# Feed-forward first: the order of TensorE's work in the steps shared by attention and feed-forward

## The reference

```
x = x + cross_attention(layernorm(x), ctx, ctx)       # 16 heads of 8
l = layernorm(x)
e = argmax(l @ Wr.T + br)                             # one of 8 experts for each token
x = x + (relu(l @ W1[e].T + b1[e]) @ W2[e].T + b2[e]) # 128 -> 512 -> 128
```

## Time and profile before

| what | us |
|---|---|
| median of 3 runs | 507.33 (504.11 to 508.76) |
| the profiled execution | 510.14 |
| its span | 508.3 |
| TensorE busy | 464.8 (91%) |
| VectorE busy | 408.4 (80%) |
| ScalarE busy | 314.4 (62%) |
| GpSimd busy | 240.2 (47%) |

### The profile page before, as it was taken

One profiled execution on the slowest core, in us unless ns is written; L12 is line 12 of the kernel. 1 busy time (PEld: TensorE's weight loads), 2 busy tenths in 40 slices (PEclk: granted clock), 3 DMA queues, 4 the chain that ended last, 5 costly groups with the idle time before them and its releaser, 6 DMA issues.

```text
span 508.3 us, 18979 instructions
## 1 busy us (share of the span) xinstructions
PE 464.8 (91%) x6467; PEld 349.6 (69%) x6468; DVE 408.4 (80%) x1061; ACT 314.4 (62%) x589; POOL 240.2 (47%) x390
## 2 busy tenths in 40 slices
PE   3999968899999999999999999979796989999991
PEld 1665634466666666666666666669686989999991
DVE  4999864678899998999989989878674768777871
ACT  1777755666656666666666666566464667767770
POOL 1558521222232845727447275357575444544552
PEclk9999997999999999999999999999998999999996
DMA  8455300001110211102111039132222322222220
GB/s 276 126 153 149 88 8 16 16 16 22 21 19 17 55 27 35 46 17 50 33 30 50 18 76 373 39 84 64 59 71 65 86 80 69 65 58 72 62 58 0
DMA packets 32745, 33.89 MB, mean 67 GB/s; under 512 B 6675, under 2 KB 26006, under 8 KB 32416
## 3 DMA queue, kind: packets, MB, share of 16 engines
q1 hardware_dynamic: 27840, 24.10, 18.0%
q0 software_dynamic: 4832, 8.80, 5.2%
HBM read 19.14 MB, written 9.99 MB: 57 GB/s over the span
## 4 chain that ended last, share of the span: by engine, by line
PE 58%; DVE 14%; issue 10%; DMA 3%; SPq 2%; ACT 2%; POOL 1%; DVEq 0%; POOLq 0%; ACTq 0%
PE PS L916 10%; PE PS L875 10%; PE PS L1022 10%; PE PS L1035 9%; PE PS L992 5%; PE PS L1001 4%; DVE MX L696 4%; PE PS L946 2%; PE PS L950 2%; PE PS L957 2%; PE PS L1007 1%; PE PS L905 1%; DMA BIG<-rows 1%; ACT PT L527 1%; DVE RD L700 1%
## 5 line engine op out<-in xcount | busy, mean ns | idle before, releaser
L449 POOL TENSOR_TENSOR VP<-BIG,C 128x128 f32<-128x128 f32 x128 | 56.3, 463 | 132.8 <-PE PS L1001 128.4
L696 DVE TENSOR_REDUCE MX<-PS 128x16 f32<-128x1024 f32 x64 | 78.3, 1223 | 28.7 <-PE PS L875 27.4
L916 PEld LDWEIGHTS PS<-C,SB 128*128 128x128 f32 x512 | 54.4, 142 | 67.9 <-ACT SB L544 32.4
L471 POOL DMA_INDIRECT out<-SB,BIG x71 | 70.0, 985 | 64.5 <-DVE SB L847 57.9
L916 PE MATMUL PS<-C,SB 128*128 128x128 f32 x512 | 84.8, 289 | 7.6 <-ACT PT L527 7.2
L544 ACT ACTIVATE SB<-SB 128x1024 f32<-128x1024 f32 x64 | 67.7, 1057 | 23.1 <-DVE SB L704 21.5
L1022 PE MATMUL PS<-BIG,KM 128*128 128x128 f32 x568 | 80.7, 282 | 0.7 <-issue 0.2
L704 DVE TENSOR_TENSOR SB<-PS,MX 128x1024 f32<-128x1024 f32 x64 | 77.4, 1210 | 1.7
L1035 PE MATMUL PS<-KM,SB 128*128 x568 | 76.1, 277 | 0.6 <-ACT SB L561 0.6
L1022 PEld LDWEIGHTS PS<-BIG,KM 128*128 128x128 f32 x568 | 71.6, 193 | 3.8 <-issue 3.1
L464 POOL DMA_INDIRECT rows<-X,DESTI x64 | 63.7, 995 | 22.3 <-issue 15.5
(11 more groups left out here) (123 smaller groups left out, 694.0 us busy)
## 6 DMA issues: line engine op xcount, KB each, us to landing
BIG<-rows SPq DMA_DIRECT2D x71, 66.0 KB
X<-in_x SPq DMA_DIRECT2D x16, 256.0 KB, 3.3
PT<-in_ctxT SPq DMA_DIRECT2D x16, 256.0 KB, 2.9
KM<-BIG SPq DMA_DIRECT2D x240, 16.0 KB
BIG<-in_we SPq DMA_DIRECT2D x1, 2576.0 KB, 10.2
KM<-in_w SPq DMA_DIRECT2D x1, 2048.0 KB, 14.6
out<-SB,BIG POOLq DMA_INDIRECT x71, 2.3
rows<-X,DESTI POOLq DMA_INDIRECT x64
```

The lines of the kernel that those rows point to most:

```text
L449: last = nc.gpsimd.tensor_tensor(dst, v, own, ALU.mult)
L471: nc.gpsimd.indirect_dma_start(out=out, out_offset=bass.IndirectOffsetOnAxis(ap=RT[:, s.r, ID:ID + 1].bitcast(i32), axis=0), in_=YO[:, s.r ...
L696: nc.vector.tensor_reduce(MX[:, n % 2, :], sc, axis=AX.X, op=ALU.max).then_inc(mx_done, 1)
L916: last = nc.tensor.transpose(bank(4)[:, i * P:(i + 1) * P], SB[:, n % 3, hp * P:(hp + 1) * P], ident)
```

## The change

In the loop over the shared steps TensorE's two calls are exchanged. The wait for the last reciprocals (`rd_done`) stays ahead of the feed-forward part of k = 2. Other engines' programs are the same.

```
@@ -1046,10 +1046,10 @@
             pe.wait_ge(tab_ready, 1)
             for n in range(F0, STEPS):
                 k = n - F0
-                stage2(Step(n // ST, n % ST, ST))
                 if k == 2:
                     pe.wait_ge(rd_done, NG)
                 ffn(0)(Step(k // RR, k % RR, RR))
+                stage2(Step(n // ST, n % ST, ST))
             steps(pe, STEPS - F0, NB1, RR, ffn(0))
```

## The result

The changed kernel takes 515.86 us (512.78 to 518.55, 6 runs), the kernel before 507.54 (503.83 to 508.76, 6 runs): ratio 1.017, 95% interval 1.0131 to 1.0209. A second series gave 515.72 against 506.68, ratio 1.0185 (1.0147 to 1.0224). The forecast was 514.9 us and a ratio of 1.015.

A forecast was written before the change was run, and what follows sets the result against it. TensorE was taken as the bound in steps 69 to 74, with DEST of step 77 gating the end. Terms 2.5 + 7.1 - 2.0 gave +7.6 us on the 507.33 median: 514.9 us, range 512.2 to 517.8, 8 in 10 508.5 to 518.7.

The forecast's parts named there:

- TensorE is the bound in steps 69 to 74: From 341.50 to 354.40 us TensorE is busy 12.90 of 12.90 us and nobody makes it wait.
- DEST is the point that counts: VectorE's DEST of step 77, the last routing batch, gates DESTI, home(10), load 18 and the blocks behind.
- Term 1: Steps 69 to 72: turns where TensorE and VectorE wait for each other take 17.57 us instead of 10.48, +7.1 us.
- the ring: Shared steps 69 to 72: L946, OT, RN, L836, relu, W2, next L946 wait in turn; 3.92 us per odd step.
- Term 2: Step 68, getting into the ring: T(1) and W1(0) come ahead of OT's counting matmuls; step 69's L946 is later, +2.5 us.
- Term 3: From step 73, getting out of the ring: pauses vanish, -3.69, but two waits partly remain; -2.0 us, between -3.7 and -1.1.
- +7.6 goes through to the end: Behind the last routing batch: DEST's whole delay of +7.6 us reaches the kernel's end through home(10) and load 18.
- the wait for block 18 stays near 3 us: Sign at TensorE behind the shared steps: its 3.12 us wait for block 18 stays about the same.
- the absorbed rival: TensorE's waits for blocks 17 and 18 take up delay if load 18 hangs elsewhere; 7.6 becomes 3.4, 510.7 us; chance 0.10.
- The clock rival: Clock falls to 1.2 GHz in the ring, steps 69 to 76: +11 us more, 526 us; chance 0.06.
- The signs: Steps 69 to 72: TensorE busy about two thirds, OT 4 us apart; home(10) near 388.4; pauses of steps 75 to 77 gone.

The follow-up runs named there:

- e8: Kernel before plus four unused VectorE copies ahead of the feed-forward part of steps 70 to 73; RN(0) to DEST 31.02 us against 30.73.
- e5: Changed kernel with VectorE adding the bias of block k-1 instead of k-2 in shared steps; 525.32 us, ratio 1.0328.
- e4: Kernel before with feed-forward first on TensorE only in steps 73 to 80; 508.64 us, ratio 1.0008.
- e11: Kernel before up to step 74; from step 75 T and W1 ahead of the step's waits, W2 behind; 505.17 us, ratio 0.9966.
- e6: Changed kernel with GpSimd writing home(k-3) ahead of the step's routing work instead of behind it; 514.59 us, ratio 1.0133.
- e7: Changed kernel plus four unused VectorE copies ahead of the feed-forward part of steps 70 to 73; RN(0) to DEST 45.78 us against 39.76.
- e10: Changed kernel with only W2 ahead of the step's own products, T and W1 behind them; RN(0) to DEST 42.72 us in one profile.
- e3: Kernel before with feed-forward first on TensorE only in steps 67 to 72; 514.09 us, ratio 1.0103.

## Why the prediction was right, point by point

- **TensorE is the bound in steps 69 to 74 and DEST is the point that counts**: held. e8's cheap copies show the first, the step from DEST to DESTI to home(10) the second (+9.04, +8.8). Over all fourteen profiles RN(0) to DEST runs from 28.9 to 48.1 us, while T(32) follows DEST by 49.0 to 53.4 us in each.
- **Term 1, the ring, +7.1**: 17.63 us against 17.57 forecast, +7.15. The links were right within 0.1 to 0.2 us, and that they add up to within 0.06 is luck: W2 to the next product was 0.99 us in each turn and not 0.89, relu of step 72 began 0.1 late, and the table arithmetic and the turn without L946 took 0.2 to 0.3 less than forecast. The sentence that T and W1 "end before relu does, so they add nothing" was wrong: they were put at about 1.0 us from RN's start on and took 1.75 (0.40 to T, 0.16 to W1, 1.19 to W2), as much as the way over L836 and relu. That made no difference to term 1, but e5 failed on it.
- **Term 2, +2.5**: step 69's L946 came 340.73 - 331.52 = 9.21 us behind RN(0) instead of 6.49, +2.7. The delay of OT was 5.74 - 4.54 = 1.20 us, as forecast, though no row shows the restart of 0.2 in it by itself; the 0.2 that was missing is W1 of step 69, which ended behind relu.
- **Term 3, -2.0**: wrong in size. From the first product of step 73 to the end of DEST it is 12.92 us instead of 13.75, -0.8, outside my bounds of -3.7 and -1.1, and done alone it even costs 1.1 (e4). I took the 3.69 us of pauses as something that vanishes and charged two turns at two thirds; pauses of 0.60, 0.67 and 0.60 us stayed, and the turns cost more than both in full (-1.1). TensorE waited there for results that VectorE hands over after its own feed-forward part, and W2 ahead of the counting delays the very next result. With only T and W1 in the pauses the gain is real, -1.84 (e11).
- **"+7.6 goes through to the end"**: wrong. DEST moved by 9.0, the end by 5.6 and 5.7 in the profiles at full clock. The load of block 18 got faster by 1.6 to 2.1 us, for a reason that I did not settle (3.92 and 3.45 before, 1.83 and 1.86 after). The clock, which fell behind the wait for block 18 before (W1 1.92 us; waits of 3.12 and 2.60 us), stayed up behind the shorter wait (1.19 and 1.12); that the shorter wait is why is not shown, as in e11 it stayed up behind 2.62. What should have been as it was, "the wait for block 18 stays near 3 us", was not. So a third of the loss was given back, but not as the absorbed rival had it: load 18 came late by all of the 8.8 us.
- **The clock rival**: I gave 0.06 to a clock that falls in the ring in every execution. It falls in some: one of three profiles of the changed kernel, and those of e5, e6, e7 and e10. The nearest row was the stretch with three pauses of 1.0 to 1.45 us at 1.00; a pause of 0.9 to 1.8 us in every step is another case. It brought +4.1 where it happened in the changed kernel. With one execution in three that lifts the +5.7 to +7.0, about half of the way to the timed +8.3 and +9.0.
- **The signs**: TensorE's share in the ring, OT 4 to 5 us apart and a late home(10) came about as written. W2 does not show a wait for relu in the changed kernel, as W1 ends with relu; it does in e10. The pauses of steps 75 to 77 shrank and did not go.

The forecast of 514.9 is therefore near for the right mechanism and with errors that offset: 1.4 us too little at DEST, 3.4 us given back that I had not seen, and a clock term on top. That the median came within 1 us of it is luck. How often the clock falls in the ring was not measured.

## What to carry to other kernels

When two in-order engines hand work to each other in both directions within a step, ask of each order what stands ahead of the first handover: the same instructions ran at 2.7 to 3.0 us a step where TensorE handed over first and worked on behind it, and at 4.2 to 4.9 us where it worked first. A pause of the busiest engine is not time to be had by itself: fill it with what nobody waits for next (T and W1, -1.8 us), not with everything that is ready (+1.1 us). Count a change in a pipeline to the point that gates the end, and then again from there, since waits behind it shrink and the clock moves with them.

## What was unexpected of the hardware

- The granted clock can fall to its 1.2 GHz level with no pause over 1.8 us: 0.68 over 10 us in one execution and 1.00 in the same stretch of two others of the same kernel. The same matmul group then takes 1.91 us instead of 1.06, or 1.33 with its late register load.
- A register load in the middle of W1 is free where TensorE had not waited (1.06 us a group, steps 69 to 73 before) and costs about 0.27 us where it has just waited (1.33 in the ring); without the load W1 takes 1.06 behind such a wait too (step 68).
- The same load of 66 KB took 3.92 and 3.45 us in two executions of one order and 1.83 and 1.86 in two of the other (e3 1.93, e4 3.00). Why is open.
